# Rebuilding the start and the first batch of a fused adaLN attention and FFN kernel: queues, groups and order

## The reference

```
mod = (silu(c) @ wmod)            # (4,512) @ (512, 6*512) -> sa, ca, ga, sb, cb, gb, one row per batch
ga, gb = sign(g) * max(|g|, 0.25)
h = layernorm(x) * (1 + ca) + sa
x = x + ga * (softmax(q k^T / sqrt(128)) v @ Wo + bo),   q, k, v = h @ Wqkv + bqkv
h = layernorm(x) * (1 + cb) + sb
x = x + gb * (h @ W_up^T + lora_B[e] @ (lora_A[e] @ h)),  e = argmax(h @ gate_w^T + expert_bias)
```

## Time and profile before

| | |
|---|---|
| median of three runs | 200.53 us |
| the profiled execution | 200.85 us |
| its span, first to last instruction | 199.0 us |
| mean granted clock of TensorE | 0.986 of full speed |
| TensorE busy | 179.0 us |
| VectorE, ScalarE, GpSimd busy | 135.2, 89.2, 80.6 us |

### The profile page before, as it was taken

How to read it: one execution, slowest core, us unless ns; L and a number is a source line. 1 busy time by engine, 2 the same in 40 slices (tenths; PEclk the granted TensorE clock), 3 DMA queues, 4 the chain that set the end, 5 groups by cost and what they waited for, 6 DMA issues and landing times.

```text
span 199.0 us, 2793 instructions
## 1 busy us (share of the span) xinstructions
PE 179.0 (90%) x933; PEld 138.0 (69%) x933; DVE 135.2 (68%) x329; ACT 89.2 (45%) x168; POOL 80.6 (41%) x104
## 2 busy tenths in 40 slices
PE   6897999899981969998999999999999999997990
PEld 6554755786751947786888789878877888675760
DVE  2828719884778697697895478659576475975443
ACT  2054045941581719832737587013565602572110
POOL 3571200059624492052296960015695000614242
PEclk9999999999999799999999999999999999999997
DMA  5999979114250000400011700000331000001204
GB/s 164 313 346 406 332 252 378 49 67 133 78 191 21 3 0 2 158 0 0 7 53 53 202 12 0 0 0 0 109 130 28 2 0 3 30 24 53 105 21 189
DMA packets 12885, 19.47 MB, mean 98 GB/s; under 512 B 3352, under 2 KB 3864, under 8 KB 12872
## 3 DMA queue, kind: packets, MB, share of 16 engines
q1 hardware_dynamic: 12872, 19.31, 28.0%
HBM read 15.09 MB, written 4.21 MB: 97 GB/s over the span
## 4 chain that ended last, share of the span: by engine, by line
PE 47%; ACT 2%; DVE 2%; issue 1%; DVEq 0%
PE bank L336 32%; PE bank L543 2%; PE bank L449 2%; PE bank L476 2%; PE bank L503 1%; ACT h2hi L799 1%; PE bank L506 1%; PE bank L484 1%; PE bank L434 1%; PE bank L428 1%; PE bank L431 1%; PE bank L405 1%; DVE xs L1273 1%; PE bank L523 1%; ACT xn_p L780 1%
## 5 line engine op out<-in xcount | busy, mean ns | idle before, releaser
L336 PE MATMUL bank<-wup_lo,h2hi 128*128 128x512 f32 x64 | 26.6, 416 | 0.0
L1326 POOL TENSOR_TENSOR rstd<-var_eps,neg_half 128x1 f32<-128x1 f32 x16 | 8.8, 552 | 43.7 <-DVE var_eps L1088 43.7
L336 PE MATMUL bank<-wup_hi,h2hi 128*128 128x512 f32 x64 | 25.2, 394 | 0.0
L336 PE MATMUL bank<-wup_hi,h2lo 128*128 128x512 f32 x64 | 25.2, 394 | 0.0
L780 ACT ACTIVATE xn_p<-xs,shift,rstd 128x512 f32<-128x512 f32 x16 | 13.1, 818 | 24.8 <-POOL shift L1329 24.8
L1341 POOL TENSOR_TENSOR xs<-xs,f_gb 128x512 f32<-128x512 f32 x15 | 19.2, 1293 | 10.9 <-DVE f_gb L1138 10.9
L336 PE MATMUL bank<-h1lo,wqkv_hi 128*128 128x512 f32 x48 | 19.8, 412 | 1.4 <-DVE h1lo L1016 1.4
L1318 POOL TENSOR_TENSOR xs<-xs,gabo 128x512 f32<-128x512 f32 x16 | 20.2, 1299 | 0.1
L336 PE MATMUL bank<-h1hi,wqkv_hi 128*128 128x512 f32 x48 | 19.0, 395 | 0.0
L336 PE MATMUL bank<-h1hi,wqkv_lo 128*128 128x512 f32 x48 | 18.9, 394 | 0.0
L1303 POOL TENSOR_TENSOR wo_ga<-wo_raw,ga_bc 128x512 f32<-128x512 f32 x4 | 5.2, 1288 | 28.1 <-DMA ga_bc<-gates_dram 28.1
(11 more groups left out here) (167 smaller groups left out, 411.3 us busy)
## 6 DMA issues: line engine op xcount, KB each, us to landing
out_dram<-xs SPq DMA_DIRECT2D x16, 256.0 KB, 2.0
xs<-in_L_attn_x_dram SPq DMA_DIRECT2D x3, 1024.0 KB, 5.2
xs<-in_L_wmod_dram SPq DMA_DIRECT2D x3, 1024.0 KB, 8.7
xs<-in_L_attn_x_dram SPq DMA_DIRECT2D x4, 256.0 KB, 3.3
stage<-in_L_wmod_dram SPq DMA_DIRECT2D x4, 256.0 KB, 5.4
xs<-in_L_wmod_dram SPq DMA_DIRECT2D x4, 256.0 KB, 5.6
stage<-in_L_wmod_dram SPq DMA_DIRECT2D x1, 1024.0 KB, 12.1
f_gb<-in_L_ffn_W_up_dram SPq DMA_DIRECT2D x1, 1024.0 KB, 5.3
```

Source lines behind the costliest of these rows:

```text
L336: mm = nc.tensor.matmul(dst, w, m, start=first and i == 0, stop=last and i == total - 1)
L1326: nc.gpsimd.tensor_tensor(rstd[:, 1, t:t + 1], var_eps[:, 1, t:t + 1], neg_half[:, 0:1], ALU.pow).then_inc(S["ln2_rstd"], 1)
```

## The change

It rewrites batch 0 and the work beside it, up to where the loop over the later batches begins. The code of that loop is the same, but for the bank numbers.

- The section ca is one DMA of 1 MB on ScalarE's queue, ahead of ScalarE's table load; sa is one DMA, and stands between the halves of Wqkv. On SP x of batch 1 and ga follow, then (once ca is used) sb, Wo, bo, W_up; then (once sa is used) x of batch 2, the gate and lora weights; then (once ga and sb are used) cb and gb; then the gate's way through DRAM.
- The first norm of batch 0 is shared: ScalarE scales tiles 0 to 2, with a shift that GpSimd makes, and VectorE tile 3.
- TensorE turns all four tiles before it multiplies ca. The result of ca is copied, turned and summed in two halves, in two banks.
- ga and sb share one bank, and so do cb and gb: two pieces of a section are accumulated in each quarter, so that a pair needs as many products as two sections did, one copy and four transposes.
- W_up is turned, and split, before the out projection and the residuals of batch 0. The gate and lora_B transposes stand before the third part of batch 1's qkv. The last part of that qkv stands behind `x2_transposes(0)`.
- VectorE and ScalarE get new orders to match.

```diff
-SEQ = ("ca", "sa", "ga", "sb", "cb", "gb")
+GROUPS = (("ca",), ("sa",), ("ga", "sb"), ("cb", "gb"))
...
-        raw = {"ca": stage, "sa": xs[:, 2], "ga": xs[:, 3], "sb": stage, "cb": xs[:, 2], "gb": xs[:, 3],
+        raw = {"ca": stage[:], "sa": xs[:, 2], "ga": xs[:, 3], "sb": stage[:], "cb": stage[:], "gb": xs[:, 3],
...
-            load_first("ca")
-            for kt in range(NK):
-                sp.dma_start(raw["wqkv"][:, kt, 0:3 * D], wqkv[kt * P:(kt + 1) * P, :]).then_inc(wqkv_in[kt], 16)
-            load_first("sa")
+            load_wqkv((0, 1))
+            load_section("sa")
+            load_wqkv((2, 3))
...
+            load_section("ga")
+            wait_used(0)
+            load_section("sb")
...
+            sp.dma_start(raw["wup"][:], wup.rearrange("(o p) h -> p o h", p=P)).then_inc(wup_in, 16)
+            wait_used(1)
+            sp.dma_start(xs[:, 2], x_v[2]).then_inc(x_in[2], 16)
...
+            wait_used(2)
+            load_section("cb")
+            load_section("gb")
             write_gate(0)
...
+                for more in range(len(GROUPS[g])):
+                    for i, (s, kt) in enumerate(quarters):
+                        mm = nc.tensor.matmul(dst[i * QUARTER:(i + 1) * QUARTER, :], silu_wide[:, kt + more, :],
+                                              raw[s][:, kt + more, :], start=more == 0, stop=more == len(GROUPS[g]) - 1)
...
-            first_x1_transposes((0,))
-            modulation("ca", (0,))
-            first_x1_transposes((1,))
-            modulation("ca", (1,))
-            first_x1_transposes((2,))
-            modulation("ca", (2, 3))
-            first_x1_transposes((3,))
-            modulation_columns("ca")
-            keep_warm(bank[4], 5)
+            first_x1_transposes(range(NT))
+            modulation(0)
+            first_modulation_columns(0)
+            first_modulation_columns(1)
+            keep_warm(bank[5], 4)
             qkv(0, (0,))
-            modulation("sa")
+            modulation(1)
             qkv(0, (1,))
-            modulation_columns("sa")
+            modulation_columns(1)
             qkv(0, (2,))
             qkv_shift_rows()
-            modulation("ga")
             qkv(0, (3,), (0,))
             qkv_shift_columns()
             qkv(0, (3,), (1, 2))
-            modulation_columns("ga")
+            modulation(2)
             scores(0)
             v_transposes(0)
-            modulation("sb")
+            modulation_columns(2)
+            p_transposes(0, (0, 1))
             gate_to_rows("ga")
-            p_transposes(0)
-            modulation_columns("sb")
+            p_transposes(0, (2, 3))
             x1_transposes(1)
             pv(0)
+            w_up_transposes(range(NK))
             qkv(1, (0,))
-            modulation("cb")
             out_projection(0)
             qkv(1, (1,))
-            modulation_columns("cb")
-            w_up_transposes((0, 1))
-            qkv(1, (2,))
-            modulation("gb")
-            w_up_transposes((2, 3))
-            qkv(1, (3,))
-            modulation_columns("gb")
+            modulation(3)
             gate_transposes()
             lora_b_transposes()
+            qkv(1, (2,))
+            modulation_columns(3)
             x2_transposes(0)
+            qkv(1, (3,))
             ffn_shift()
...
+            nc.scalar.dma_start(raw["ca"], wmod_v[SECTION["ca"]]).then_inc(mod_in["ca"], 16)
             act.wait_ge(S["cT_psum"], 1)
...
             pt_high(0)
             h1_high(1)
+            o_high(0)
+            wup_high((0, 1))
             wo_high(0)
-            o_high(0)
-            modulation_rows("cb")
+            wup_high((2, 3))
             ln2_normalise(0, (0, 1))
...
             h2_high(0)
+            qkv_evacuate(1)
             wo_high(1)
+            ln1_normalise(2)
             act.wait_ge(S["fb_psum"], 1)
...
             gz_evacuate(0)
-            ln1_normalise(2)
...
             qk_low(0)
+            maxima(0)
             add_parts("ga")
             gate_columns("ga")
-            maxima(0)
+            v_low(0)
+            pt_low(0, (0,))
             gate_rows_evacuate("ga")
-            v_low(0)
-            pt_low(0)
+            pt_low(0, (1, 2, 3))
             add_parts("sb")
+            h1_low(1)
             split_sb()
-            h1_low(1)
...
             o_low(0)
-            residual(0, 0)
-            ln2_moments(0, 0)
-            residual(0, 1)
-            ln2_moments(0, 1)
-            add_parts("cb")
-            scale_columns("cb")
...
             wup_low(range(NK))
-            ln1_stats(2, (0, 1, 2, 3))
-            ln1_moments(2)
-            qk_low(1)
-            add_parts("gb")
+            for t in range(NT):
+                residual(0, t)
+                ln2_moments(0, t)
...
+            add_parts("cb")
+            scale_columns()
+            add_parts("gb")
+            ln1_stats(2, (0, 1, 2, 3))
+            ln1_moments(2)
             h2_low(0)
+            qk_low(1)
             gate_columns("gb")
             ffn_shift_rows()
             gate_shift()
```

More of the change, by code:

```diff
@@ L355, in modulation_columns, with modulation @@
[L355 to L358, removed]
+            def modulation(g):
+                dst = open_bank("mod", g)
+                for s in GROUPS[g]:
+                    pe.wait_ge(mod_in[s], 16)
+                if g == 0:
+                    pe.wait_ge(S["silu_step"], 4)
+                quarters = [(s, kt) for s in GROUPS[g] for kt in range(0, NK, len(GROUPS[g]))]
+                for more in range(len(GROUPS[g])):
+                    for i, (s, kt) in enumerate(quarters):
+                        mm = nc.tensor.matmul(dst[i * QUARTER:(i + 1) * QUARTER, :], silu_wide[:, kt + more, :],
+                                              raw[s][:, kt + more, :], start=more == 0, stop=more == len(GROUPS[g]) - 1)
+                mm.then_inc(S["mod_psum"], 1)
@@ new lines, in first_modulation_columns, with modulation_columns @@
+            def first_modulation_columns(half):
+                pe.wait_ge(S["mod_rows_ready"], half + 1)
+                dst = open_bank("caT", half)
+                for nt in (2 * half, 2 * half + 1):
+                    mm = nc.tensor.transpose(dst[:, nt * P:(nt + 1) * P], mod_rows[:, 0, nt * P:(nt + 1) * P], ident[:])
+                mm.then_inc(S["modT_psum"], 1)
+            def modulation_columns(g):
+                pe.wait_ge(S["mod_rows_ready"], g + 2)
+                dst = open_bank("modT", g)
@@ L442, in v_transposes, with p_transposes @@
                 mm.then_inc(S["V_psum"], 1)
-            def p_transposes(b):
-                for t in range(NT):
+            def p_transposes(b, tiles=range(NT)):
+                for t in tiles:
                     dst = open_bank("PT", b, t)
@@ L933, in add_parts @@
             def add_parts(s):
-                i = SEQ.index(s)
-                dve.wait_ge(S["modT_psum"], i + 1)
-                parts = at("modT", s)[:].rearrange("p (n k r) -> p n r k", n=NK, k=NK)[:, :, 0:B, :]
-                nc.vector.tensor_reduce(mod_sum[:, i, :].rearrange("p (n b) -> p n b", n=NK), parts, AX_X,
-                                        ALU.add).then_inc(S["mod_sum_ready"], 1)
+                g = next(i for i, group in enumerate(GROUPS) if s in group)
+                n, i = len(GROUPS[g]), GROUPS[g].index(s)
@@ new lines, in add_parts, with first_columns @@
+                dve.wait_ge(S["modT_psum"], g + 2)
+                parts = at("modT", g)[:].rearrange("p (n s q r) -> p n s r q", n=NK, s=n, r=QUARTER)[:, :, i, 0:B, :]
+                nc.vector.tensor_reduce(mod_sum[:, SEQ.index(s), :].rearrange("p (n b) -> p n b", n=NK), parts, AX_X,
+                                        ALU.add).then_inc(S["mod_sum_ready"], 1)
+            def first_columns():
+                for half in range(2):
+                    parts = at("caT", half)[:].rearrange("p (n q r) -> p n r q", n=NK, r=QUARTER)[:, :, 0:B, :]
+                    nts = slice(2 * half, 2 * half + 2)
+                    total = mod_sum[:, 0, half * 2 * B:(half + 1) * 2 * B].rearrange("p (n b) -> p n b", n=2)
+                    dve.wait_ge(S["modT_psum"], half + 1)
+                    nc.vector.tensor_reduce(total, parts[:, nts], AX_X, ALU.add).then_inc(S["mod_sum_ready"], 1)
+                    dve.wait_ge(S["mod_sum_ready"], half + 1)
+                    nc.vector.tensor_scalar(modT["ca"][:, nts, :], total, 1.0, None, ALU.add).then_inc(S["modT_ready"], 1)
+                dve.wait_ge(S["modT_ready"], 2)
```

170 lines of the change are left out of this document (77 added, 93 removed), and 6 rows, old and new, of the table order.

## The result

The changed kernel took 198.77 us in the median, beside 200.98 for the kernel before (20 runs each); the ratio is 0.9874, with a 95% interval of 0.9853 to 0.9894. The forecast was 194.5 with a range of 192.4 to 198.2, so the time lies outside. The profiled execution took 198.70 us with a span of 197.0, where 200.85 and 199.0 stood before.

The account below looks back on a forecast made before the run. TensorE was taken to bound the kernel, busy 179.0 of 199.0 us. Start 0.0, 5.3 saved up to the gate product, 6.0 in all by batch 1's softmax: 200.85 - 6.0 = 194.85, as a median 194.5; range 192.4 to 198.2.

Parts of the forecast that it names:

- The start: Batch 0 up to qkv's first product: 0.9 saved on ca's chain, taken back by x's later arrival; net 0.0 us.
- The upper bound: Batch 0 up to qkv's first product: ca is served ahead of x, +1.4 us.
- the lower bound: Batch 0 up to qkv's first product: x is not delayed and the halves hide ca's copy wholly, -1.5 us.
- The clock in the start: Rival: TensorE's clock drops to 1.2 GHz before batch 0's qkv, costing 2.4 us, so 196.9; chance 0.17.
- The wait of 4.7 and the half clock behind it: TensorE's wait ahead of the gate transposes becomes 0.9, full clock returns; -5.3 us up to the gate product.
- The gate's way: Batch 0's gate rows copied 1.7 us later, first residual 2.8 later at 49.9; wait ahead of `pv` 2.1.
- Behind it: Gate product to batch 1's last softmax tile: TensorE waits 0.6 for VectorE's gate sums; -6.0 us in all.
- x not delayed: Rival: at the start ca fits in beside x on the DMA engines, gaining 0.9, so 193.6 us; chance 0.17.
- The gate behind cb and gb: Rival: gate's way through DRAM queues behind these two sections, spread gate lands 3.4 later, so 197.9 us; chance 0.10.
- VectorE stays late: Rival: five small steps between residuals and h2 take 1.05 each, chain 4.3 longer, so 198.8 us; chance 0.07.
- W_up ahead of Wo's high part: Rival: a late W_up DMA holds ScalarE's Wo part and TensorE's batch 1 qkv; slower, 203 us; chance 0.05.
- The norm's place: ScalarE's norm of batch 2, now before the lora rows' copy, not between gz and softmax: saving 5.3 to 6.0.

Follow-up runs that it names:

- filler: The changed kernel with 24 filler products (keep_warm) instead of 8 ahead of the first tile's transposes: 197.08 us, ratio 0.9801.

## Why the prediction was wrong

**The start: wrong, and this is the step that failed.** The prediction took 0.0 for it, with bounds -1.5 and +1.4. It measured +3.3. It assumed that ca and x share the DMA engines from the first byte on, so that x's last tile lands late and its first ones hardly. The rule it weighed (a second queue is not more bandwidth) was right and not sharp enough. Half of ca went before x's first byte, and the first tile of x, not the last, was what everything waited for: 6.90 against 3.62 on VectorE's timeline. The upper bound named this case ("ca is served first") and priced it well: with filler, so at full clock, qkv started at 17.80, 1.5 later than before. The other 1.8 are the clock. The run with ca behind x shows the lower bound: -1.6. The prediction's own sign of being wrong, a wait over 2.5 us that it doesn't name, stands in the profile with 2.9.

**The clock in the start: a rival, right in kind, and the other half of the miss.** It was given 0.17 and a gap near 1 us in each 1.5. The idle piece was 2.9 in one, since x's lateness made it. It cost 1.8 us by the filler run, where 2.4 was taken. The prediction gave the upper bound and this rival each a place in its range, but not both together: 194.5 + 1.4 + 2.4 is 198.3, just over the range's end of 198.2. In fact the late tile made the gap. A late tile did not bring the fall each time: with ca moved on the kernel before, TensorE stood idle for 2.0 us and kept 1.00; with ca first on SP, idle pieces of 2.2 and 0.9 with four transposes between were followed by 0.50.

**The wait of 4.7 and the half clock behind it: right.** From qkv's first product to the gate product's end the forecast was 5.3 less. Before, that is 72.1 - 16.3 = 55.8; after, 70.1 - 19.6 = 50.5: 5.3 less. That it fits to the tenth is in part luck, since two misses of half a microsecond cancel in it (next paragraph).

**The gate's way: right.** The first residual was to start 33.6 us behind qkv (49.9 - 16.3). It started 33.2 behind it, in this row of the changed kernel:

```profile
52.83 0.75 DVE L1107 SCALAR_TENSOR_TENSOR xs<-bank,row_inv,xs 128x512 f32<-128x512 f32 x1 [2.33 <-POOL xs L1340]
```

The wait ahead of `pv` was forecast at 2.1 and measured at 1.6, the one for the norm at 0.9 and measured at 1.4. The new crossing at `out_projection` didn't wait.

**Behind it: right in kind, 0.4 too good.** The last softmax tile was to end 6.0 earlier by the forecast with the start unmoved; it ended at 78.36 + 0.69 = 79.05, 2.3 earlier, which is 5.6 once the start's 3.3 is taken out. The 0.4 is VectorE's gate steps: TensorE's wait behind them was to be 0.6 and is 1.4. The prediction said that three stretched steps would be hidden; in the changed kernel all four are stretched, and they end where GpSimd's operations end (69.83 and 71.09 beside 69.81 and 71.06 for the first two), so they last beyond the copy behind which they should hide. VectorE and then GpSimd in the changed kernel:

```profile
68.98 0.85 DVE L1002 SCALAR_TENSOR_TENSOR gate_tmp<-mod_sum 128x16 f32<-128x16 f32 x1
69.76 1.33 DVE L1004 TENSOR_SCALAR gate_tmp<-mod_sum 128x16 f32<-128x16 f32 x1
71.12 1.21 DVE L1007 TENSOR_SCALAR gate_tmp<-gate_tmp 128x16 f32<-128x16 f32 x1
72.37 1.20 DVE L1010 SCALAR_TENSOR_TENSOR gate_col<-gate_tmp 128x16 f32<-128x16 f32 x1
73.61 0.76 DVE L1040 SCALAR_TENSOR_TENSOR lbw<-stage,low_rows,bank 32x512 fp32r<-32x512 f32 x1
```

```profile
68.50 1.31 POOL L1330 TENSOR_TENSOR gabo<-bo_bc,ga_bc 128x512 f32<-128x512 f32 x1
69.75 1.31 POOL L1334 TENSOR_TENSOR wo_lo<-wo_ga,wo_hi 128x512 fp32r<-128x512 f32 x1
71.00 4.99 POOL L1340 TENSOR_TENSOR xs<-xs,gabo 128x512 f32<-128x512 f32 x4
```

ScalarE's copy had ended at 72.06 + 0.59 = 72.65, and the lora rows started at 73.61.

**The rivals.** x not delayed: false as the change stands. The gate behind cb and gb: false, Wo's product on GpSimd began at 45.54, 4.8 after the gate rows were copied at 40.74, where it was 5.0 before. VectorE stays late: false, its small steps between the residuals and h2 took 0.17 to 0.19, and the only wait there is the one for the norm. W_up ahead of Wo's high part: no lateness. The norm's place, the step from 5.3 to 6.0: shown, and worth some 2.1 us.

**The sum.** -5.6 and +3.3 make -2.3 at the softmax, and -2.15 at the end of the profiled executions (200.85 to 198.70); the rest, 0.15, is within what TensorE's wait for o's low part in batch 1 grew by (0.8 to 1.2). With ca behind x the same code gives 194.09, beside the forecast 194.5. Part of that agreement is one error against another. The start is 1.6 earlier, which the forecast did not have, and 0.85 is lost behind it: the softmax's last tile ends at 74.14, 7.2 earlier and so 5.65 without the start, where 6.0 was forecast, and another 0.5 goes behind it, where the wait for o's low part grew from 0.8 to 1.5. The forecast also starts from the median of three runs, 200.53, where twenty have 200.98: its saving of 6.0 taken off that is 195.0.

Two of the prediction's figures don't follow from its own terms: its bounds come to 193.0 and 196.4 (written 192.8 and 196.3), and W_up at 53 would give 203.9 (written 203). Neither bears on the forecast.

## What to carry to other kernels

Ask of an early transfer what it is served ahead of: a megabyte that nobody needs for 10 us, issued 0.4 us before the tile on which everything hangs, cost 4.4 us here (198.48 to 194.09), and moving it back made the rest of the change worth about what was forecast. When a part of the change makes an engine late at the start, cost a fall of TensorE's clock together with the lateness, not as an independent rival: here the lateness alone was 1.5 over the old start and both were 3.3. And a wait on a busy helper engine is not repaired by moving its last releaser; look at what else stands on that engine's list, small steps beside another engine's large ones above all.

## What was not expected of the hardware

- Two DMA queues shared only late: x's first tile, 256 KB issued at 1.21 us on SP's queue, had moved nothing by 4 us, while 0.52 MB of ca (issued at 0.79 on ScalarE's) had. It was seen at 6.90, and at 7.10 with both on one queue.
- A VectorE step over 4 elements took 2.35 us and ended with a run of four GpSimd sums, through the change from the third to the fourth; in other kernels the same step took 0.23 beside the same sums, where it started 0.1 us ahead of that change.
- TensorE's clock fell to 0.50 after 2.9 us of idleness in the changed kernel, and after pieces of 2.2 and 0.9 with ca first on SP; it stayed at 1.00 after 2.0 us in the profiled execution of the kernel before with ca moved.
